# Causal attention: bfloat16 thirds of q and k replaced by float32r halves on 64-row tiles, in a written order

## The reference, cut to what matters

```python
q = split_heads(x @ Wq + bq); k = split_heads(x @ Wk + bk); v = split_heads(x @ Wv + bv)
scores = einsum('bhqd,bhkd->bhqk', q, k) / sqrt(16)
scores = where(causal, scores, -inf)
attn = softmax(scores, axis=-1)
x = layernorm(x + einsum('bhqk,bhkd->bhqd', attn, v) @ Wo + bo)
x = layernorm(x + shared_expert(x) + two_of_sixteen_experts(x))
```

## Time and profile before

| what | value |
|---|---|
| device time, median of 3 runs (lowest, highest) | 1043.27 us (1041.78, 1044.07) |
| span of the profiled execution, first to last instruction | 975.7 us |
| the profiled execution's own time | not stated by the profile; the median lies 67.6 us above the span |
| stage 1, about | 0 to 118 us |
| stage 2, about | 118 to 607 us |
| stage 3, about | 607 to 976 us |
| PE / DVE / ACT / POOL busy | 88% / 68% / 49% / 31% of the span |
| granted TensorE clock, mean | 0.943 |

### The profile page before, as it was taken

The page is one execution under the profiler, slowest core; times in us unless marked ns, Lnnn a source line. Parts: engine busy times, 40 slices in busy tenths (PEclk is TensorE's granted clock), DMA queues, the critical chain, the costliest instruction groups (busy, mean ns, idle before and its releaser), DMA issues. The chain is left out here.

```text
span 975.7 us, 18404 instructions
## 1 busy us (share of the span) xinstructions
PE 854.0 (88%) x5476; PEld 478.9 (49%) x5477; DVE 660.1 (68%) x1527; ACT 476.2 (49%) x686; POOL 300.0 (31%) x368
## 2 busy tenths in 40 slices
PE   7979799999999989999999997799898999999300
PEld 4635434444444434444444432687556777777200
DVE  6428688888888887888888870489892122466364
ACT  3423266656666656656666566455322444444100
POOL 3423312211112111221112211442477500464373
PEclk9979899999999999999999999889899999999755
DMA  8773855444764266425754000710126745766443
GB/s 285 193 205 131 162 67 75 100 97 59 131 85 89 36 117 118 68 38 106 130 66 57 9 2 25 235 65 23 60 103 210 232 137 152 207 207 211 157 126 95
DMA packets 82464, 113.95 MB, mean 117 GB/s; under 512 B 8945, under 2 KB 60401, under 8 KB 82417
## 3 DMA queue, kind: packets, MB, share of 16 engines
q1 hardware_dynamic: 57808, 78.01, 38.1%
q0 software_dynamic: 6720, 18.88, 5.9%
q10 hardware_dynamic: 17888, 16.41, 5.2%
HBM read 62.55 MB, written 50.33 MB: 116 GB/s over the span
## 5 line engine op out<-in xcount | busy, mean ns | idle before, releaser
L658 ACT ACTIVATE work<-ps 128x1024 f32<-128x1024 f32 (+3 forms) x384 | 293.8, 811 | 185.5 <-PE ps L725 185.3
L335 DVE TENSOR_REDUCE m_neg<-ps 128x1 f32<-128x512 f32 (+3 forms) x432 | 265.6, 662 | 29.2 <-PE ps L320 18.7
L629 POOL TENSOR_SCALAR_AFFINE_SELECT work<-work 128x512 f32<-128x512 f32 x128 | 81.2, 634 | 394.4 <-ACT work L658 390.0
L317 PE MATMUL ps<-stacks 96*128 96x512 bf16 (+3 forms) x528 | 151.9, 332 | 1.5 <-DVE m_neg L335 1.5
L725 PE MATMUL ps<-stacks 99*128 99x512 bf16 (+3 forms) x528 | 124.6, 329 | 6.4 <-PEq L371 4.8
L335 DVE TENSOR_REDUCE m_neg_late<-ps 128x1 f32<-128x384 f32 (+3 forms) x176 | 106.7, 636 | 27.4 <-PE ps L320 27.4
L740 PE MATMUL ps<-work,vg 128*32 128x512 f32 (+3 forms) x1056 | 112.5, 498 | 1.6 <-POOL work L629 1.6
L320 PE MATMUL ps<-mask_b,ident_b 128*128 128x128 bf16 x512 | 100.3, 223 | 0.0
L317 PEld LDWEIGHTS ps<-stacks 96*128 96x128 bf16 x528 | 50.0, 98 | 95.0 <-DVE m_neg L335 48.8
L1243 DVE TENSOR_TENSOR work<-work,ps 128x256 f32<-128x256 f32 x48 | 20.2, 421 | 106.7 <-ACT work L1062 106.7
L1421 PE MATMUL ps<-wgu,work 128*128 x384 | 91.7, 382 | 0.3 <-issue 0.3
(11 more groups left out here) (143 smaller groups left out, 1098.4 us busy)
## 6 DMA issues: line engine op xcount, KB each, us to landing
stacks<-qk_parts SPq DMA_DIRECT2D x132, 128.0 KB, 6.3
qk_parts<-work SPq DMA_DIRECT2D x32, 384.0 KB, 3.0
y_sorted<-work SPq DMA_DIRECT2D x8, 1536.0 KB, 9.9
work<-y_sorted SPq DMA_DIRECT2D x48, 256.0 KB
z_sorted<-work ACTq DMA_DIRECT2D x48, 256.0 KB
wgu<-qk_parts SPq DMA_DIRECT2D x60, 128.0 KB, 6.5
work<-in_xT SPq DMA_DIRECT2D x8, 512.0 KB, 4.8
work<-in_x SPq DMA_DIRECT2D x8, 512.0 KB, 3.6
```

The source lines that it names most:

```text
L317: mm = pe.matmul(dst, qs[r][0:KS, h0 + m, qt * P:(qt + 1) * P], ks[r][0:KS, h0 + m, half * CH:half * CH + w], start=True, stop=not diag)
L335: dve.tensor_reduce(dst, ps[:, bank, 0:heads * w].rearrange("p (h k) -> p h k", h=heads), AX.X, ALU.max, negate=True).then_inc(reduced, 1)
L629: pool.affine_select(out=blk_, in_=blk_, compare_op=ALU.is_ge, fill=0.0, base=0, pattern=[[0, GH], [1, P]], channel_multiplier=-1).then_in ...
L658: act.activation(probs[:, s + 2 * pair:s + 2 * pair + 2, off:CH], ps[:, SCORE_BANK + 2 * pair:SCORE_BANK + 2 * pair + 2, off:CH], ACT.Exp, ...
```

## The change

- q and k are split into two float32r parts (high, and the rest) instead of three bfloat16 parts. `PRODUCTS` has three products: a head has 48 contracted rows, and 50 with the maximum in two parts. ACT's second activation and POOL's subtraction in stage 1 are gone.
- Two heads lie in one stack, one in partitions 0 to 63 and one in 64 to 127. The matmuls of the two follow each other and use different row halves of TensorE and different banks. The masks become two matmuls for each head (of 128 and of 64 columns), as each half of the rows can only take half of the identity; `ident_x` and `mask_x` hold the halves exchanged.
- Maxima pieces take a pair of banks and two or four heads: 20 pieces instead of 38, each reduced by one DVE instruction. The two narrowest units of qc=0 share one bank pair and one exponential: 11 units.
- Banks 0 to 5 are three slots of two banks which scores and maxima pieces take in turn; bank 6 collects the outputs, bank 7 takes all transposes. `ORDER_OF_STEP` is written out; `weigh` follows two units behind the scores instead of one.
- `max_parts` moves from DVE to POOL (two instructions instead of four); DVE keeps the combination of the two halves. The maxima are turned by one float32 transpose instead of four bfloat16 ones. `load_max` issues four DMAs instead of three, `load_stacks` 18 instead of 12.
- TensorE's 16 steps are unrolled. `wgu` and `yT_all` get memory of their own after the attention.

```diff
-PRODUCTS = [(0, 0), (0, 1), (1, 0), (0, 2), (2, 0), (1, 1)]
-KM = KS + 3
-UNITS = [(qc, kt) for qc in range(HALVES) for kt in range(CT * (qc + 1))]
+PRODUCTS = [(0, 0), (0, 1), (1, 0)]
+KM = KS + 2
+ROWS = 64
+PAIRED = GH // 2
+LOADS = 16 * len(PRODUCTS) * 2 * (PAIRED + 1)
+UNITS = [(0, [(0, 0, 0)]), (0, [(1, P, P)]), (0, [(2, 2 * P, 2 * P), (3, 3 * P, P)])]
+UNITS += [(1, [(kt, off, off)]) for kt, off in enumerate([0] * CT + [P * j for j in range(CT)])]
...
-        heads = 4 if w == P else 2 if w == 2 * P else 1
-        MAXES += [(qt, h, heads, half, w) for h in range(0, GH, heads)]
+        heads = 2 if w <= 2 * P else 1
+        MAXES += [(qt, h, heads, half, w) for h in range(0, PAIRED, heads)]
...
-RING = [4, 5, 7]
+SLOTS = 3
+OUT_BANK, TURN_BANK = 6, 7
+WEIGH_BEHIND = 2
+ORDER_OF_STEP = (
+    "m0 s0a m1 s0b w-2 m2 s1a t1 s1b w-1 m3 s2a m4 s2b o1 s3a m5 m6 w0 s3b w1 m7 s4a t0 m8 s4b m9 w2 m10 "
+    "s5a m11 s5b m12 w3 s6a m13 s6b o0 s7a m14 w4 m15 s7b m16 w5 s8a m17 w6 s8b m18 s9a w7 s9b s10a m19 "
+    "w8 s10b"
+)
+RING_USERS = [item for item in ORDER if item[0] in ("scores", "max")]
+TURNS = [item for item in ORDER if item[0] in ("turn_max", "turn_out")]
+def slot_bank(item):
+    return 2 * (RING_USERS.index(item) % SLOTS)
...
         def load_stacks(sp, i, r):
             for n, (qp, kp) in enumerate(PRODUCTS):
...
+                for x in range(2):
+                    rows = slice(x * ROWS + n * DK, x * ROWS + (n + 1) * DK)
+                    for a in range(PAIRED):
+                        sp.dma_start(qs[r][rows, :, a].bitcast(F32),
+                                     q_rows[x][:, a].rearrange("d (c t) -> d c t", c=HALVES))\
+                            .then_inc(stack_loaded[r], 16)
+                    sp.dma_start(ks[r][rows].bitcast(F32), k_rows[x]).then_inc(stack_loaded[r], 16)
...
         def piece_scores(pe, i, r, n, bank):
+            qt, p0, pairs, half, w = MAXES[n]
+            diag = half == qt // CT
+            for m in range(pairs):
+                dst = [ps[:, bank + x, m * w:(m + 1) * w] for x in range(2)]
+                for x in range(2):
+                    rows = slice(x * ROWS, x * ROWS + KS)
+                    mm = pe.matmul(dst[x], qs[r][rows, qt // CT, p0 + m, qt % CT * P:(qt % CT + 1) * P],
+                                   ks[r][rows, p0 + m, half * CH:half * CH + w], start=True, stop=not diag)
                 if diag:
-                    mm = pe.matmul(dst[:, w - P:w], ident_b[:, :], mask_b[:, :], start=False, stop=True)
+                    for j in range(2):
+                        for x in range(2):
+                            rows = slice(x * ROWS, (x + 1) * ROWS)
+                            one, low = (ident_b, mask_b) if j == x else (ident_x, mask_x)
+                            mm = pe.matmul(dst[x][:, w - P + j * ROWS:w], one[rows, :], low[rows, j * ROWS:P],
+                                           start=False, stop=j == 1)
...
         def turn_maxima(pe, i, qc, bank):
             pe.wait_ge(m_ready[qc], i + 1)
+            pe.transpose(ps[:, bank, 0:P], m_parts[:, qc].bitcast(F32), ident[:, :]).then_inc(mT_ready[qc], 1)
...
+        def both_halves(dve, i):
+            dve.wait_ge(reduced, NM * i + NM)
+            dve.tensor_tensor(m_neg[:, 1], m_neg[:, 1], m_late[:, :, :, :], ALU.min).then_inc(m_both, 1)
+        def max_parts(pool, i, qc):
+            high = m_parts[:, qc, 0:GH * CT]
+            low = m_parts[:, qc, GH * CT:2 * GH * CT]
+            m = m_neg[:, qc].rearrange("p x a t -> p (x a t)")
...
+            pool.tensor_copy(high, m).then_inc(m_step, 1)
+            pool.wait_ge(m_step, done + 1)
+            pool.tensor_tensor(low, m, high.bitcast(F32), ALU.subtract).then_inc(m_ready[qc], 1)
         def load_max(sp, i, r, qc):
             sp.wait_ge(mT_copied[qc], i + 1)
-            for part in range(3):
+            for part in range(2):
+                for x in range(2):
...
                 for r in range(STACKS):
-                    dve.memset(ks[r][KS:KM], 1.0).then_inc(ones_ready, 1)
+                    for x in range(2):
+                        dve.memset(ks[r][x * ROWS + 32:(x + 1) * ROWS].bitcast(F32), 1.0).then_inc(stack_ones, 1)
...
                 def step(i, r, more=True):
-                    for u in DIAG[:CT]:
-                        mask(i, u)
+                    max_parts(pool, i, 1)
+                    for u in DIAG[:ND0]:
+                        mask(i, r, u)
                     if more:
                         wait_count(pool, pv_done, NU * (i - 1))
                         values(pool, i + 1, (r + 1) % STACKS)
+                        max_parts(pool, i + 1, 0)
...
+                def scores(i, r, u, pair, first, last):
+                    qc, parts = UNITS[u]
+                    bank = slot_bank(("scores", u, pair))
+                    if pair == 0 and u in (0, NU0):
+                        pe.wait_ge(m_loaded[qc], 64 * i + 64)
+                    slot_free(i, ("scores", u, pair), first, last)
+                    for kt, off, at in parts:
+                        for x in range(2):
+                            rows = slice(x * ROWS, x * ROWS + KM)
+                            mm = pe.matmul(ps[:, bank + x, at:at + CH - off], ks[r][rows, pair, kt * P:(kt + 1) * P],
+                                           qs[r][rows, qc, pair, off:CH], start=True, stop=True)
...
-                with pe.Fori(0, 4) as j:
-                    for q in range(STACKS):
-                        step(STACKS * j + q + 2, j + (q + 2) // STACKS, (q + 2) % STACKS)
+                for i in range(STEPS):
+                    if i == 2:
+                        pe.wait_ge(ones_ready, STACKS)
+                    step(i, i // STACKS, i % STACKS, first=(i == 0), last=(i == STEPS - 1), second=(i == 1))
```

More of the change, by code:

```diff
@@ L8 @@
 BF16 = mybir.dt.bfloat16
+F32R = mybir.dt.float32r
 I32 = mybir.dt.int32
@@ L53, with first_column @@
 STACKS = 3
-RING = [4, 5, 7]
-def unit_width(u):
-    qc, kt = UNITS[u]
-    return CH - max(0, P * (kt - CT * qc))
-def attention_order():
[L67 to L88, removed]
+SLOTS = 3
+OUT_BANK, TURN_BANK = 6, 7
+def first_column(u):
+    return min(at for _, _, at in UNITS[u][1])
+WEIGH_BEHIND = 2
[4 more added lines that the diff above has]
+)
+def attention_order():
+    what = {"s": "scores", "m": "max", "w": "weigh", "t": "turn_max", "o": "turn_out"}
+    order = []
+    for word in ORDER_OF_STEP.split():
+        pair = "ab".index(word[-1]) if word[0] == "s" else 0
+        order.append((what[word[0]], int(word[1:].rstrip("ab")), pair))
+    assert sorted(n for w, n, _ in order if w == "max") == list(range(NM))
+    assert sorted(n for w, n, _ in order if w == "weigh") == list(range(-WEIGH_BEHIND, NU - WEIGH_BEHIND))
     return order
@@ L107, in present, with slot_before @@
     return not (first and item == ("turn_out", 1, 0))
-def ring_before(item, first, last, second=False):
-    at = RING_USERS.index(item) - len(RING)
+def slot_before(item, first, last):
+    at = RING_USERS.index(item) - SLOTS
     while at >= 0:
@@ L115, in ring_before, with turn_before @@
             return RING_USERS[at], 0
-        at -= len(RING)
+        at -= SLOTS
     if first:
         return None, 0
-    at += len(RING_USERS)
-    while not present(RING_USERS[at], second, False):
-        at -= len(RING)
-    return RING_USERS[at], 1
+    return RING_USERS[at + len(RING_USERS)], 1
+def turn_before(item, first, last, second=False):
+    at = TURNS.index(item) - 1
+    while at >= 0:
+        if present(TURNS[at], first, last):
+            return TURNS[at], 0
+        at -= 1
+    if first:
+        return None, 0
+    at += len(TURNS)
+    while not present(TURNS[at], second, False):
+        at -= 1
+    return TURNS[at], 1
 EARLY = [("max", n) for n in range(NM)]
 EARLY.insert(NM0 + TURN_AFTER, ("turn_max", 0))
-EARLY_BANKS = [6, 7]
+EARLY_BANK = 6
 EARLY_CHUNKS = 3
@@ L371, in build @@
         with ExitStack() as c1:
             xt = [piece(1024 * i, DC, CH) for i in range(2)]
-            rest = [piece(2048 + 512 * t, CH) for t in range(4)]
-            parts = [piece(4096 + 768 * t, 768).bitcast(BF16).rearrange("p (r t) -> p r t", r=3) for t in range(4)]
+            parts = [piece(2048 + 1024 * t, 2, CH).bitcast(F32R) for t in range(4)]
             xt_loaded = [sem(f"xt_loaded{i}") for i in range(2)]
@@ L768, in step @@
                         if item == ("max", 0, 0) and not last:
[L769 removed]
+                            pe.wait_ge(stack_loaded[(r + 1) % STACKS], LOADS * (k3 + (r + 1) // STACKS) + LOADS)
                         if what == "scores":
[L771 removed]
+                            scores(i, r, n, pair, first, last)
                         elif what == "weigh":
```

295 lines of the change are left out of this document (135 added, 160 removed).

## The result

The changed kernel is slower: 1100.36 us (1097.05 to 1104.49) against 1043.17 us for the kernel before on the same chip, ratio 1.0546 [1.0507, 1.0584]. The prediction was 977 us, range 930 to 1035. The loss of 57 us lies in stage 2.

A forecast was written before the change was run, and what follows sets the result against it. TensorE's stream of work was taken as the bound: a stage 2 step falls from 30.81 to 26.1 us, 70.7 us less over fifteen periods, last step 1.0 less, stage 1 +5, giving 977 us, range 930 to 1035.

The forecast's parts named there:

- Work, 23.8: TensorE's new sum per stage 2 step: matmuls, masks, weighs, transposes and tile-shape switches, 23.8 us without waits.
- Wait (b): Stage 2, unit 3: TensorE stands for the qc=1 maxima's transpose, copy and DMA chain, 0 to 2.3 us, taken as 1.2.
- Wait (a): Stage 2: scores and maxima pieces share three slots, so TensorE waits for the slower of DVE and ACT, 1.1 us per step.
- rival B: Stage 2: shared slots and the maxima chain eat the gain; step 29.0 us, kernel 1021 us, chance 0.15.
- Wait (c): Stage 2: `max_parts` on POOL stands behind the last unit's mask; about 2.2 us, hidden by 0.5 us.
- DVE, 22.8: DVE's busy time per stage 2 step falls from 26.6 to 22.8 us through fewer instructions.
- Unrolling, 0.2 per step: Stage 2: unrolling removes the 2.87 us idle time at a loop's return, 0.2 us per step.
- The last step, 1.0 less: End of stage 2, filled by ACT: three slots feed it more evenly, 23.3 us instead of 24.3.
- Stage 1, +5: Stage 1: more stack loads and memsets before the attention add 5 us, range 0 to 10.
- C: Rival for stage 2: the row halves do not overlap; step 34.0 us, kernel 1096 us, chance 0.08.
- D: Rival for stage 2: float32r is streamed at float32's pace; step 48.8 us, kernel 1324 us, chance 0.09.
- A: Rival for stage 2: both engines full, DVE becomes the bound; step 23.4 us, kernel 933 us, chance 0.21.

The follow-up runs named there:

- after: The changed kernel, unedited, against the kernel before on the same chip: 1100.36 us against 1043.17 us, ratio 1.0546.
- both edits: Changed kernel with score pair s3a two places later and maxima loaded by two DMAs instead of four: 1022.98 us, ratio 0.9798 to the kernel before.
- spare work: Changed kernel with eight useless float32r matmuls in front of the wait for the loaded maxima: 1007.14 us, ratio 1.0334 to the kernel before.
- order edit: Changed kernel with score pair s3a moved two places later in TensorE's written order: 964.92 us, ratio 0.9883 to the kernel before.
- loop version: Changed kernel with s3a two places later and TensorE's inner steps in a loop again instead of unrolled: ratio 1.0043 to the kernel before.

## Why the prediction was wrong

**The failed step** is the clock. The prediction added two new waits and priced them by their length, on the ground that the last step "with its waits still has 1.00". The last step's idle times stand elsewhere and in another mix; the row could not carry that. The trace of before held a sign of it, in stage 2 itself: behind the 2.87 us of the earlier trace rows the clock falls to 0.70, and that step takes 34.94 us where its neighbours take 30.36, so 1.7 more than the idle time.

```profile
364.00:368.00 4.00, 2.28 (x12) 1.44 (x13) 0.88 (x4) 1.02 (x1) 0.00 (x0) 0.70 0.02 4
```

In after the waits cost themselves and then, in eight steps, 10 us and more at half speed. That makes up most of the 42.4 us, and the last step's clock of 0.79 takes more: 32.8 against 27.7 in the version with both edits. It is shown by the spare work (same period, clock restored); the masks left out agree (less work, longer waits, clock lost). Which steps lose the clock stays open, as the same waits stand in steps that keep it.

**The period at full clock** is the second miss: 31.2 instead of 26.1, outside the bounds of 23.4 to 29.9.
- *Work, 23.8.* Measured 26.5 with reductions halved. The distances from each matmul's start to the next, without idle time, take the step from 202.7 of that run apart: score and piece pairs 13.2, with the changes of tile shape behind them, where the prediction had 9.0 and 1.7 for all changes; masks 2.1 (2.4), weighs 9.2 (9.4), transposes 1.8 (1.25). So the term that failed is the pairs. The prediction bounded a pair of 512 by the longer of its stream (0.215) and two loads (0.214). Back to back that comes out, at 0.228. In the step most take 0.33 to 0.34, about the stream and one load together, so the sum of 10.3 for both kinds, taken as the upper bound, was too low. Why the load hides behind like pairs and not in the step is not shown; waits that are met and increments are not the reason. The Trainium skill ("TensorE: Matmul & The Clock Gate", LDWEIGHTS) has 1.2 GHz for a load's columns, 0.107 us; the 0.108 of a pair of 128 columns agrees, with the two loads side by side.
- *Wait (b), 1.2.* Itself 1.12 to 1.28 in 14 of the 15 steps, and its chain 4.8 us where 5.0 was the bound: right. Missing was what it drags along: s3b takes the slot of s3a and stands for its exponential, another 1.24 for ACT. Moving s3a two places took both, 2.0 us of the period.
- *Wait (a), 1.1.* The 1.3 that it started from was what the prediction's own sum left over: TensorE idles 0.1 us in the step of before. The period of 30.81 holds two odd steps, of 32.7 and 34.9 us; the 13 others are 30.3 to 30.4. In after the rest of the idle time in a full-clock step, 4.1 in all less 2.4, is 1.7 us, and halved reductions take 0.9 of idle time from the version with both edits. Near rival B in kind ("the shared slots and the maxima chain"), whose 29.0 us was also too short, and whose 1021 us knows nothing of the clock.
- *Wait (c), none:* right; the transpose of the maxima (191.96) has no idle time in front, and POOL's two instructions take 0.19 and 0.22.
- *DVE, 22.8:* 23.6 measured, as a reduction of 1024 elements takes 1.22 instead of 1.15. *ACT* 19.5, as said.
- *Unrolling, 0.2 per step:* worth 1.6% with the order edit, mostly by the clock.

**The last step, 1.0 less:** to the last reciprocal it is 25.1 before, 32.0 after and 26.9 with both edits, so three slots did not shorten it. **Stage 1, +5:** +0.9 here, and +3.2 between the two profiles on the second chip (the first marker at 116.49 and 119.72). The loads of the first set did take longer to issue, from 38.15 to 49.44, but TensorE's wait for xT became 5.14 us where 7.29 stood. **Stage 3, 0:** right.

**The rivals.** C's 1096 us lies close to the result and is wrong: the halves do overlap. D is wrong as well. A needed the order that hides the chain, and TensorE's work alone rules out its 23.4. No case had a lowered clock in it, although the text named one as what would make it wrong, and so the range ended at 1035 us. C and D together have 0.17, so the 0.16 given for slower was a slip.

## What to carry to other kernels

When TensorE is full and a change leaves it less work in the same order, look first at the idle times that this opens. Here two of some 1.2 us in a step took some 40 us out of 510 through the clock, beside the 2.4 us of each step that they are themselves. Price a matmul among the neighbours that it will have: the float32r pair of 0.228 us back to back took 0.34 in the step. Move the work that waits for a chain of small steps (transpose, copy, DMA) behind work that waits for nothing, and count what stands behind it on the shared slots; here one word moved in an order written by hand turned 5% slower into 1% faster, and two DMAs in place of four made it 2%.

## What the hardware showed that was not expected

- TensorE ran at clock 0.50 from about 48 to 92 us in the kernel of matmuls alone, though it was busy all the time, nearly all of that time with matmuls on one row half (0.43 us from start to start for 512 columns of 50 rows). It rose some 5 us into the bfloat16 pairs on both halves, to 0.93 in the stretch from 92 to 96. No wait stood there, so what lowers the clock is not idle time alone.
- Steps with the same waits come out at either clock: 196.76 (1.00) and 259.27 (0.77) in after, and in the loop version 217.72 (1.00) and 308.78 (0.94), both with 0.48 us for the maxima's DMA.
- The first step of the changed kernel had full clock in no version: 0.65 in after, 0.79 to 0.81 in those with the order edit.
